# Rows of a slot six partitions apart in the stacked keys and queries of a cross-attention

## What is computed

```python
q = (query @ Wq + bq).reshape(B, Nq, H, D).transpose(0, 2, 1, 3)      # H = 16 heads, D = 16
k = (key_value @ Wk + bk).reshape(B, Nkv, H, D).transpose(0, 2, 1, 3)  # Nkv = 12544
v = (key_value @ Wv + bv).reshape(B, Nkv, H, D).transpose(0, 2, 1, 3)
attn = jnp.einsum('bhqd,bhkd->bhqk', q, k) * scale
attn = jax.nn.softmax(attn, axis=-1)
x = jnp.einsum('bhqk,bhkd->bqhd', attn, v).reshape(B, Nq, Cq)
```

## Time and profile before

| | |
|---|---|
| median of three runs | 1377.11 us |
| the profiled execution | 1377.1 us |
| its span, first to last instruction | 1375.0 us |
| mean granted TensorE clock | 0.918 of full speed |
| TensorE (PE) busy | 1212.0 us, 88% |
| VectorE (DVE) busy | 715.2 us, 52% |
| ScalarE (ACT) busy | 714.6 us, 52% |
| GpSimd (POOL) busy | 224.6 us, 16% |

### The profile page before, as it was taken

One profiled execution on the slowest core, in us unless ns is written; L12 is line 12 of the kernel. 1 busy time (PEld: TensorE's weight loads), 2 busy tenths in 40 slices (PEclk: granted clock), 3 DMA queues, 4 the chain that ended last, 5 costly groups with the idle time before them and its releaser, 6 DMA issues.

```text
span 1375.0 us, 29487 instructions
## 1 busy us (share of the span) xinstructions
PE 1212.0 (88%) x12749; PEld 779.0 (57%) x12749; DVE 715.2 (52%) x1351; ACT 714.6 (52%) x995; POOL 224.6 (16%) x118
## 2 busy tenths in 40 slices
PE   8799999999999989316799989999999999989566
PEld 6256666566655656216598345666565666656344
DVE  2546555455555553568223526555555555555342
ACT  3246666666666657242213346666666666657322
POOL 0222222222222200033000212222222111210000
PEclk9689999999999999657799779999999999999769
DMA  8969777767776680610804969777777777790440
GB/s 150 138 82 123 94 93 95 99 84 97 98 96 91 76 174 3 208 64 0 306 1 76 131 84 118 97 95 97 97 90 97 92 99 102 82 151 7 170 159 5
DMA packets 80947, 138.18 MB, mean 100 GB/s; under 512 B 9064, under 2 KB 72176, under 8 KB 80304
## 3 DMA queue, kind: packets, MB, share of 16 engines
q1 hardware_dynamic: 79920, 136.16, 63.5%
q10 hardware_dynamic: 896, 0.12, 0.1%
HBM read 57.96 MB, written 0.15 MB: 42 GB/s over the span
## 4 chain that ended last, share of the span: by engine, by line
PE 73%; DVE 17%; DMA 4%; issue 2%; ACT 2%; POOL 0%; SPq 0%; ACTq 0%; DVEq 0%; POOLq 0%
PE ring L543 39%; PE st L543 17%; PE ot L543 15%; DVE mpart L1221 8%; DMA qst<-rowb 4%; DVE arena L1348 2%; PE ring L674 1%; DVE arena L1352 1%; ACT arena L932 1%; PE ring L549 0%; DMA warena<-ctxT 0%; PE ring L642 0%; DVE work L1342 0%; POOL arena L532 0%; DVE work L1296 0%
## 5 line engine op out<-in xcount | busy, mean ns | idle before, releaser
L1221 DVE TENSOR_REDUCE mpart<-ring 128x1 f32<-128x448 f32 x896 | 516.5, 620 | 441.5 <-PE ring L543 439.4
L955 ACT ACTIVATE work<-st 128x1024 f32<-128x1024 f32 x392 | 400.8, 1022 | 199.5 <-PE st L543 195.3
L543 PE MATMUL ring<-arena,qst 96*128 96x448 bf16 x896 | 300.5, 370 | 4.9 <-DVE mpart L1221 1.9
L543 PE MATMUL st<-qst,arena 97*128 97x128 bf16 x3136 | 244.7, 221 | 22.2 <-DMA qst<-rowb 21.1
L543 PE MATMUL ot<-work,arena 128*17 128x128 f32 x6272 | 250.3, 277 | 8.5 <-issue 6.4
L543 PEld LDWEIGHTS st<-qst,arena 97*128 97x128 bf16 x3136 | 198.5, 98 | 86.9 <-DMA qst<-rowb 32.8
L543 PEld LDWEIGHTS ot<-work,arena 128*17 128x17 f32 x6272 | 138.6, 97 | 150.9 <-issue 104.0
L495 POOL TENSOR_TENSOR arena<-arena 128x896 f32<-128x896 f32 x52 | 98.1, 1887 | 720.9 <-ACT arena L928 720.9
L543 PE MATMUL ring<-warena,wkv 96*128 96x448 f32 x448 | 195.8, 567 | 2.0 <-DVE mpart L1221 1.3
L543 PE MATMUL ring<-wkv,warena 96*128 96x256 f32 x784 | 192.8, 389 | 1.1 <-DVE mpart L1221 1.0
L543 PEld LDWEIGHTS ring<-wkv,warena 96*128 96x128 f32 x784 | 149.4, 194 | 29.1 <-DVE mpart L1221 11.0
(11 more groups left out here) (278 smaller groups left out, 624.9 us busy)
## 6 DMA issues: line engine op xcount, KB each, us to landing
arena<-arena SPq DMA_DIRECT2D x336, 224.0 KB, 11.3
warena<-ctxT SPq DMA_DIRECT2D x28, 672.0 KB, 13.4
arena<-ffn_W SPq DMA_DIRECT2D x16, 1024.0 KB, 12.4
arena<-f SPq DMA_DIRECT2D x2, 4096.0 KB, 24.3
arena<-scratch_bc SPq DMA_DIRECT2D x1, 2048.0 KB, 7.1
arena<-rows SPq DMA_DIRECT2D x1, 1792.0 KB, 7.0
warena<-w_in_proj SPq DMA_DIRECT2D x1, 1024.0 KB
warena<-w_W SPq DMA_DIRECT2D x1, 1024.0 KB, 13.8
```

The source lines that it names most:

```text
L543: return nc.tensor.matmul(o, l, r, start=start, stop=stop, **kw)
L955: nc.scalar.activation(pbuf[:, n % 2], st[:, 2 * (n % 2):2 * (n % 2) + 2].rearrange("p b k -> p (b k)"), ACT.Exp).then_inc(*signal(f"{lay} ...
L1221: V.reduce_max(mpart[:, 2 * h + hf:2 * h + hf + 1], ring[:, BANKS[step][0], 0:HALF], AX_X).then_inc(*signal(f"{lay}_b_max"))
```

## The change

Row l of slot s, for l from 0 to 15, lay in partition 16 s + l. Now it lies in partition 6 l + s. A DMA of a slot writes 16 partitions that are six apart, over nearly the whole height of the 96, instead of 16 neighbours. Keys and queries are changed alike, so each row still meets its partner; the sum over the 96 rows is taken in another order. Number, sizes, sources and order of all DMAs and of all other instructions stay as they were.

```diff
@@ stack(lay, c)
                         for s in range(SLOTS):
                             if K_SPLIT[s] == part:
-                                load(kst[HD * s:HD * (s + 1), b].rearrange("l (h m) k -> l h m k", m=KC)[:, :, m],
+                                load(kst[s:SLOTS * HD:SLOTS, b].rearrange("l (h m) k -> l h m k", m=KC)[:, :, m],
                                      kparts[:, part, m * CK:(m + 1) * CK], f"{lay}_kst{m}_in")
@@ attention_loads(lay, later_weights)
                 for s, part in enumerate(Q_SPLIT):
-                    load(qst[HD * s:HD * (s + 1), 0].rearrange("l (h m) t -> l h (m t)", m=KC),
+                    load(qst[s:SLOTS * HD:SLOTS, 0].rearrange("l (h m) t -> l h (m t)", m=KC),
                          qparts[:, part].rearrange("p m t -> p (m t)"), f"{lay}_qst_in")
```

## The result

The changed kernel takes 1338.46 us in the median of four runs (1334.81 to 1340.97), the kernel before 1376.96. The ratio is 0.9721, with a 95% interval of 0.9678 to 0.9764: 38.5 us less, where 20.0 were forecast, and under the low end of the range (1348). A second set of five runs gave 1338.40 us and 0.9736 (0.9721 to 0.9751). The profiled execution took 1334.81 us with a span of 1332.7.

What follows compares the result with a forecast made beforehand. It took the cross-attention to be bound by TensorE. Idleness and clock savings in L0 and L1, 5.78 + 4.22 + 5.54 + 4.50 = 20.0 us, off 1377.1 gave 1357.1 us; range 1347.7 to 1378.

Steps and rivals of the forecast that it cites:

- low end: Fastest case, 1347.7 us: 6.4 us for the stalls at the layers' ends and 3 for clock dips, beyond the forecast.
- The backlog: Start of a layer: stack loads fall from 1.85 to 1.01 us, so the row of maxima lands before TensorE needs it.
- The idleness and the clock of the first stage: First score groups of L0 and L1: TensorE's waits go (5.78, 5.54 us) and its clock stays at 1.00 (4.22, 4.50 us).
- the clock does not come back: Rival at the first score groups: only the idleness goes, 11.3 us saved, 1365.8 us; chance 0.15.
- the source or the copy itself limits: Rival: a stack load still takes 1.85 us, time 1377 us; no change, by either of two reasons, had 0.14.
- The later chunks: Chunks after a layer's start: stack loads are never waited for; the remaining ten row waits, 9.8 us, stay.
- the ends of the layers: TensorE's "issue" stalls of 3.10 and 3.29 us before 501.15 and 1233.16: may move or go, counted as 0.
- My reason for the stalls: Layers' ends: the 3.10 and 3.29 us stalls lie where weights flow at 393 GB/s behind the last stack loads.
- The row waits for something else: Rival: the row's delay is a layer's first-row cost, not backlog; 1377 us; no change, by either of two reasons, 0.14.
- Slower: Rival: scattered rows lengthen stack loads; from 2.77 us each DMA bounds every chunk, at 3.70 us 1646 us; chance 0.05.

Runs made afterwards that it cites:

- experiments 1 and 3: 1: stack loads alone, rows variously spaced: two apart 1.09 us per load, four, eight and six 1.15 to 1.19; 3: changed kernel, rows two apart: 1337.00 us.
- experiments 2 and 4: 2: kernel before, only first two chunks spread 1357.29 us, only later chunks 1358.25; 4: kernel before, half the bytes per stack load from chunk 3 on, 1356.92 us.
- Experiment 5: Kernel before, but SyncE issues the weights ending each cross-attention only after the last stack load has landed: 1382.92 us, ratio 1.0063.
- note of experiment 1: In a kernel of stack loads alone, a 4 KB DMA of another queue issued after two or eight of twelve queued loads: 4.3 to 14.5 us to land.

## Why the prediction was right in direction and too small

*The backlog.* Right, to the figure. A stack load now takes 1.06 us with changing slots, forecast 1.01; the old one 1.86 against 1.85. That the new figure came out so near is partly luck: it was borrowed from the context load because shares of that lie six apart, and experiments 1 and 3 show that six apart is nothing special. ScalarE's wait is gone: both casts of chunk 1 run at once, at 36.77 in the changed kernel, where the prediction had 36.7.

```profile
36.77 1.78 ACT L928 CAST arena<-arena 128x896 bf16<-128x896 f32 x2
```

The last context load was issued at 48.17 instead of 52.41, and the row landed in 1.7 us.

*The idleness and the clock of the first stage.* Right. The forecast was 5.78 + 4.22 and 5.54 + 4.50 = 20.0 us; the table gives 9.8 and 11.4. Of the surplus in L1, 1.05 us is that its twelve projections before the score group took 6.63 us instead of 7.68, by a clock that rose earlier; in L0 they took 7.80 instead of 7.27. The prediction had left them as they were. The kernel with only the first chunks spread measured it by itself: 18 us. The rival "the clock does not come back" fell, and so did "the source or the copy itself limits".

*The later chunks.* This is the step that failed: "stack loads are never waited for, and the row is issued when they are idle (1.7 us to land), so the remaining ten row waits stay", and with it "I count 0" for the ends of the layers. I had looked at who waits for `arena<-arena` and at the median landing of the row. Neither shows a third user of the same engines, the instruction fetch. By the times of its packets it came late behind stack loads that filled the engines, and TensorE's wait then has the name "issue". In the middle of the layers the row itself came late: that of 258.60 us was issued at 255.0 together with stack loads and ran beside a fetch packet of 255.94 to 257.23, and its own last packet came at 257.24; it landed after 3.6 us. Two stalls of 3.1 and 3.3 us, six row waits of 0.6 to 2.0 us, of which the changed kernel keeps four of 0.2 to 1.3, some gaps of 0.5 to 0.8 us, and a fall of the clock behind several of them made the 17 to 18 us that experiments 2 and 4 measured. The sum of these pieces was not worked out one by one. Of these the low end had 6.4 + 3; the row waits were left out altogether, though the maximum of 3.6 us stood beside the median in rows 7.

*My reason for the stalls* was wrong as well. They stand where the weights are issued, and I took the weights for their cause. Experiment 5 moved the weights; the stall stayed. In the changed kernel weights flow at full rate at that place, and there is no stall.

*The row waits for something else*, the rival with the Trainium skill, DMA: Bandwidth & Descriptors, section "Queues, rings and completion order", in which queues take turns at each packet, does not foretell what a small DMA meets here. The row of L0 landed in 12.5 us before and in 1.7 us after, and the note of experiment 1 waited up to 14.5 us; what holds it, the engine or the feeding of descriptors, stays open.

*Slower.* Nothing of it was seen: no wait for `arena<-arena` on TensorE.

## What to carry to other kernels

A DMA that nobody waits for can still cost time, if it fills the DMA engines: small transfers of other queues and, by all that the traces show, the fetch of instructions stand behind it, and the waits then carry other names. So compare the GB/s of a full stretch with what the same engines move elsewhere in the trace, and where it is half or less, look at how many neighbouring partitions the destination has; two apart was enough here. Read the maximum of a landing time beside its median, and count small waits and the clock dips behind them together. After such a gain look for work that can now start earlier: one reordering that cost 1.3% before the change gave 0.6% after it.

## What was not expected of the hardware

Sixteen rows one apart took 24.75 us for twelve loads with a fixed slot, and 22.33 us with changing slots; six apart 13.75 and 12.66 us. A 4 KB DMA of ScalarE's queue landed after 14.5 us behind eight loads of SyncE's queue. One instruction packet took 1.86 us in the crowd, another 0.96 us out of it. A source of 16 partitions held loads at 90 GB/s whatever the destination; why was not tried.
